# A fused attention and expert kernel: the transposed maxima of the scores go to the second score bank, one step sooner, and the expert masks ahead of the third maximum

## The reference

```
q = LN(x);  k = v = ctx;  rope(q), rope(k);  Q, K, V = 16 heads of 8
x = x + tanh(g_xattn) * (softmax(Q K^T / sqrt(8)) V Wo^T + bo)
z = LN(x);  xn = rmsnorm(z) * norm_scale;  s = xn Wr^T           # 8 experts
ids = top2(s);  c = softmax(s)[ids]
y = sum over ids of c * (up_val(xn) * silu(up_gate(xn))) Wdown^T   # hidden 352
x = x + tanh(g_ffn) * (y + z)
```

## Time and profile before

| | |
|---|---|
| median of 3 runs | 489.53 us |
| the profiled execution's own time | 488.46 us |
| its span (first to last instruction) | 486.7 us |
| granted TensorE clock, mean | 0.907 |
| TensorE busy | 395.8 us (81%) |
| VectorE busy | 300.7 us (62%) |
| ScalarE busy | 259.8 us (53%) |
| GpSimd busy | 249.0 us (51%) |

### The profile page before, as it was taken

The page is one execution under the profiler, slowest core; times in us unless marked ns, Lnnn a source line. Parts: engine busy times, 40 slices in busy tenths (PEclk is TensorE's granted clock), DMA queues, the critical chain, the costliest instruction groups (busy, mean ns, idle before and its releaser), DMA issues.

```text
span 486.7 us, 13346 instructions
## 1 busy us (share of the span) xinstructions
PE 395.8 (81%) x3788; PEld 269.2 (55%) x3789; DVE 300.7 (62%) x1112; ACT 259.8 (53%) x578; POOL 249.0 (51%) x205
## 2 busy tenths in 40 slices
PE   7578788888979788897987313999999999999960
PEld 3234445464655546455644202777777778777750
DVE  6377678788877887877773430555555555555440
ACT  3232658687676777785757301555455555545520
POOL 4464204136544565635344562456675665667574
PEclk9867899989899998998979555999999999999996
DMA  6331514037377703314011122334353443444230
GB/s 182 105 89 41 143 35 126 22 111 195 87 203 222 185 25 99 92 57 144 26 42 58 55 82 61 65 50 61 52 60 47 57 55 50 55 53 60 21 27 4
DMA packets 57413, 38.99 MB, mean 80 GB/s; under 512 B 8820, under 2 KB 55031, under 8 KB 57367
## 3 DMA queue, kind: packets, MB, share of 16 engines
q1 hardware_dynamic: 42614, 28.24, 22.0%
q0 software_dynamic: 12736, 8.64, 12.8%
q10 hardware_dynamic: 2016, 1.52, 1.2%
HBM read 14.29 MB, written 11.75 MB: 54 GB/s over the span
## 4 chain that ended last, share of the span: by engine, by line
PE 50%; DVE 16%; issue 10%; DMA 9%; ACT 4%; SPq 4%; POOL 3%; POOLq 2%; ACTq 1%; another core or an unknown queue 1%; DVEq 0%
DMA out<-ys,yi 7%; PE bank L1373 6%; PE bank L1351 6%; PE bank L1353 6%; DVE nmx L769 4%; PE bank L1176 4%; PE bank L1363 3%; SPq L237 3%; PE bank L1163 3%; PE bank L1097 2%; PE bank L1193 2%; PE bank L1150 2%; PE bank L1209 2%; ACT pt L542 2%; PE bank L1205 2%
## 5 line engine op out<-in xcount | busy, mean ns | idle before, releaser
L481 POOL DMA_INDIRECT out<-ys,yi x72 | 112.3, 1559 | 74.5 <-issue 37.1
L401 POOL DMA_INDIRECT slots_dram<-xr,slu x64 | 63.8, 997 | 69.3 <-ACT pt L542 47.5
L769 DVE TENSOR_REDUCE nmx<-bank 128x4 f32<-128x512 f32 x128 | 85.7, 676 | 11.9 <-PE bank L1150 11.5
L542 ACT ACTIVATE pt<-bank 128x512 f32<-128x512 f32 x128 | 72.9, 595 | 17.3 <-PE bank L1163 16.5
L1056 DVE TENSOR_TENSOR hh<-sg,bank 128x352 f32<-128x352 f32 x72 | 37.5, 521 | 54.3 <-PE bank L1353 39.3
L1373 PEld LDWEIGHTS bank<-wf_sb,hT 128*128 128x128 f32 (+1 forms) x432 | 56.7, 190 | 23.7 <-issue 19.8
L1373 PE MATMUL bank<-wf_sb,hT 128*128 (+1 forms) x432 | 61.0, 277 | 4.0 <-DVE hT L1066 4.0
L688 ACT ACTIVATE ys<-bank,yc 128x128 f32<-128x128 f32 x72 | 26.4, 367 | 63.7 <-PE bank L1373 33.4
L1351 PE MATMUL bank<-wf_sb,xT 128*128 x144 | 56.0, 471 | 0.0
L1176 PE MATMUL bank<-pt,v 128*9 128x128 f32 x1024 | 50.8, 282 | 6.1 <-ACT pt L542 5.3
L1353 PE MATMUL bank<-wf_sb,xT 128*128 x144 | 55.0, 464 | 0.0
(11 more groups left out here) (163 smaller groups left out, 708.2 us busy)
## 6 DMA issues: line engine op xcount, KB each, us to landing
qs<-parts SPq DMA_DIRECT2D x48, 128.0 KB
ks<-parts SPq DMA_DIRECT2D x42, 128.0 KB
xs<-slots_dram SPq DMA_DIRECT2D x72, 66.0 KB
wf_sb<-in_wup SPq DMA_DIRECT2D x8, 352.0 KB
x_sb<-in_x SPq DMA_DIRECT2D x8, 256.0 KB, 3.3
ctx_sb<-in_ctx_in SPq DMA_DIRECT2D x8, 256.0 KB
out<-x_sb SPq DMA_DIRECT2D x8, 256.0 KB
out<-ys,yi POOLq DMA_INDIRECT x72
```

What stands on the lines that cost most here:

```text
L401: nc.gpsimd.indirect_dma_start(out=slots_dram, out_offset=bass.IndirectOffsetOnAxis(ap=slu[:, c % 2, k, kk:kk + 1], axis=0), in_=xr[:, c % ...
L481: nc.gpsimd.indirect_dma_start(out=out.rearrange("b s d -> (b s) d"), out_offset=bass.IndirectOffsetOnAxis(ap=yi[:, r:r + 1], axis=0), in_ ...
L542: nc.scalar.activation(pt[:, 4 * g:4 * g + 4, :], STB[g % 2][:, :].rearrange("p (h s) -> p h s", h=4), ACT.Exp, scale=SCORE_SCALE).then_in ...
L769: nc.vector.tensor_reduce(nmx[:, b % 2, at:at + 4], SB[g % 2][:, :].rearrange("p (h s) -> p h s", h=4), AX.X, ALU.max, negate=True).then_i ...
```

## The change

The transposed maxima get another place, rows 0 to 15 and columns 0 to 127 of SB[1]. TensorE transposes the maxima of b + 2 at the end of step b, after the last weighted values and ahead of `project_out(b - 1)`, instead of those of b + 1 behind the scores near the step's start. VectorE makes the two copies right behind maximum 3 of the same batch. New waits follow: group 1 of the scores waits for the copies of the batch before (`d_mT`), and `transpose_attended` waits for `add_attention` of the batch before; the old waits of `transpose_maximum` on `add_attention` and of `transpose_attended` on `d_mT` go. SP issues the maxima of b + 2 at the end of its step. Ahead of the loop the maxima of batch 1 are transposed, copied and sent too.

On VectorE `choose_masks` and `choose_sum` (u = 0) move ahead of `maximum(b + 2, 2)`; `take_positions` and `take_scores` move ahead of `add_attention`, and `widen` (u = 3) behind it; the two copies stand ahead of `rotate_q` (u = 1).

```diff
-        mT_ps = SMALL[0:NH, 256:384]
+        mT_ps = SB[1][0:NH, 0:S]
...
 (SP)        maxima(0)
             sp.wait_ge(zeroed, 6)
+            maxima(1)
...
-                if real(b + 1):
-                    maxima(b + 1)
                 if u == 0 and there(c + 1):
                     stack_q_low(c + 1)
                     stack_k_high(c + 1)
                     stack_k_low(c + 1)
                 if 8 <= b < 8 + E:
                     ffn_weights(b - 8)
+                if real(b + 2):
+                    maxima(b + 2)
...
 (VectorE)   for g in range(4):
                 maximum(1, g)
+            maximum_high(1)
+            maximum_low(1)
...
                 if real(b + 2):
                     maximum(b + 2, 0)
-                if real(b + 1):
-                    maximum_high(b + 1)
-                    maximum_low(b + 1)
...
+                if u == 0 and there(c - 2):
+                    choose_masks(c - 2)
+                    choose_sum(c - 2)
                 if real(b + 2):
                     maximum(b + 2, 2)
-                if u == 0 and there(c - 2):
-                    choose_masks(c - 2)
+                if real(b + 2):
+                    maximum(b + 2, 3)
...
-                if u == 0 and there(c - 2):
-                    choose_sum(c - 2)
                 if real(b + 2):
-                    maximum(b + 2, 3)
+                    maximum_high(b + 2)
+                    maximum_low(b + 2)
                 if u == 1 and there(c + 2):
                     rotate_q(c + 2)
-                if u == 3 and there(c + 3):
-                    widen(c + 3)
-                if real(b - 1):
-                    add_attention(b - 1)
                 if u == 0 and there(c - 2):
                     take_positions(c - 2)
                 if u == 3 and there(c - 1):
                     take_scores(c - 1)
+                if real(b - 1):
+                    add_attention(b - 1)
+                if u == 3 and there(c + 3):
+                    widen(c + 3)
...
 (TensorE)       if 4 * b + g > 1:
                     pe.wait_ge(d_max, 4 * b + g - 1)
+                if g == 1 and b:
+                    pe.wait_ge(d_mT, b)
...
             def transpose_maximum(b):
                 pe.wait_ge(d_max, 4 * b + 4)
-                if b >= 3:
-                    pe.wait_ge(d_x1, b - 2)
...
             def transpose_attended(b):
                 pe.wait_ge(d_on, b + 1)
-                pe.wait_ge(d_mT, min(b + 3, B))
+                if b:
+                    pe.wait_ge(d_x1, b)
...
-            pe.wait_ge(d_bo, 8)
             transpose_maximum(0)
             for g in range(4):
                 scores(1, g)
+            transpose_maximum(1)
+            pe.wait_ge(d_bo, 8)
...
-                if real(b + 1):
-                    transpose_maximum(b + 1)
...
                     weighted_values(b, 3)
+                if real(b + 2):
+                    transpose_maximum(b + 2)
                 if real(b - 1):
                     project_out(b - 1)
```

## The result

The changed kernel took 503.37 us (median of 4 runs, 496.38 to 506.81); the kernel before took 489.61 us beside it. The ratio is 1.0226, with a 95% interval of 1.0159 to 1.0293: slower by some 2%, where I forecast 1.3% faster. The ratio rests on the faster runs (496.38 and 500.91); the profiled execution is a slower one, 506.81 us with a span of 505.0, so I use its trace for places and waits and not for the size of the loss.

A forecast was written before the change was run, and what follows sets the result against it. The prediction took the loop as bound by turns by TensorE and VectorE, ScalarE close behind, with about 20 us of movable TensorE waits. Its terms summed to -6.6 us off a median of 489.53: 482.9 us, range 478.5 to 490.5.

The forecast's parts named there:

- rotate_q: +1.6: VectorE, u = 1: `rotate_q` behind the copies sometimes meets GpSimd's `rotate_k`; a quarter of 6 x 1.1 us, +1.6 us.
- Rival B: GpSimd takes the gain back: `rotate_q` meets `rotate_k` in four rounds (4.4 us), no clock gain; 487.6 us, chance 0.18.
- Rival C: Each step's end: VectorE idles while TensorE transposes, 8.3 us in place of 2.8; slower, 493.9 us, chance 0.12.
- my sign of C: What would show Rival C: VectorE idle before the copies by over 8 us in total.
- The transposition (-3.8): TensorE's transposition of the maxima no longer waits for `add_attention`; half of 7.6 us comes back, -3.8 us.
- copies (-1.7): VectorE's two copies leave the step's head; half the 3.4 us scores wait for maxima comes back, -1.7 us.
- masks (-2.4): Masks ahead of the third maximum at u = 0 come sooner: 0.4 us for six rounds, -2.4 us.
- rival D: ScalarE is next: oT is ready no sooner and holds all 7.6 us and the clock; 487.8 us, chance 0.14.
- New waits (+2.8): Each step's output product queues behind maximum 3, at u = 2 behind the statistics, +2.8 us; scores 1's wait costed at nothing.
- SP's queue (-0.8): DMA issue in the loop: maxima of u = 2 leave before store and loads, so the second DMA wait goes, -0.8 us.
- Start (-1.2): Ahead of step 2: maxima of batch 2 land sooner, warming starts 0.95 us later; net -1.2 us.
- Clock (-1.1): Low-clock u = 0 steps of rounds 3 and 5: one of the two regains full clock, -1.1 us.

The follow-up runs named there:

- e4: The kernel before with only `rotate_q` moved behind `add_attention` in step u = 1: 504.10 us, ratio 1.0350.
- e1: The changed kernel with GpSimd's `rotate_k(n)` waiting until `rotate_q(n)` is done (n >= 2): 487.09 us, ratio 0.9956 to the kernel before.
- e10: e4 with GpSimd's `rotate_k` waiting for `rotate_q` as in e1: 490.34 us, ratio 1.0025 to the kernel before.
- e5: e1 with the expert weights issued in steps u = 2 and 3 of rounds 2 to 5, not steps 8 to 15: 483.23 us, ratio 0.9878.
- e2: The changed kernel with `rotate_q` put ahead of the two copies in step u = 1: 486.45 us, ratio 0.9998 to the kernel before.
- e9: The kernel before with both side edits of e5 (`rotate_k` waiting, weights moved) and nothing of the change: 487.44 us, ratio 0.9967.
- e8: e5 with `choose_masks` and `choose_sum` back behind maximum 2: 485.53 us, ratio 0.9955 to the kernel before.

## Why the prediction was wrong

**rotate_q: +1.6, the step that failed.** It failed in the start, in the price and in the reader. I wrote that `rotate_q` "starts up to 0.5 us later relative to the step". Against the output product it started 1.0 to 1.3 us later in rounds 2 to 5 (0.09 us behind it before, 1.39 in round 2 after). I priced a meeting with `rotate_k` at 1.1 us for one half, from the single meeting of before. In rounds 2 to 5 GpSimd ran both of its halves at once, and VectorE's half outlasted them: up to 3.58 us, 2.9 more than its 0.67. And I named no reader of it, though `project_q` waits for `rotate_q` directly (`d_q`) and stands in the very next step; TensorE's 12.1 us of waiting and the lower clock behind it were in no term. All six steps met, not a quarter. `rotate_q` came later by the wait for the transposition and two copies, and GpSimd's `rotate_k` 0.3 to 0.5 us sooner against the product in rounds 2 to 4 (2.0 in round 5). I took GpSimd's distance of "about a microsecond" for a property of GpSimd's; it hung on `rotate_q` being ahead of the second scatter (e4). e1, e4 and e10 show this step alone: moved without the change it costs 3.5%, and one wait on GpSimd takes the loss away from either kernel. Step 10 alone is no clean measure of it: in e1 it still takes 3.0 us more than before, behind the DMA of the maxima. Steps 14, 18 and 22 are: 12.27, 11.73 and 11.49 us in the changed kernel, 8.67, 7.43 and 8.44 in e1.

Rival B had the mechanism and too small a price (4.4 us, its ceiling 6.6), for the same reason. Rival C had the sign by the wrong mechanism. VectorE did stand idle in front of the copies (16.9 us, my sign of C was 8), but it had stood idle there for the output product before, and e5 has 14.5 us of it and is faster; the sign was a bad one.

**Who gives way.** The Trainium skill, SBUF — State Buffer, section "Who interferes with whom", was the warning, and its first half holds: two tensor inputs on VectorE against a GpSimd instruction that reads. That the one issued first keeps its way for a whole instruction (from which, too, it does not follow that `shift` would always lose, as I wrote) does not fit the starts in these rows: VectorE began 0.20 us (e4) and 0.53 us (after) before GpSimd and still finished behind two of GpSimd's instructions. The measurement decides. Other rows do fit: in round 1 of e2 the second half of `rotate_q` kept its 0.69 us and GpSimd's first took 2.01 instead of 1.27. Where VectorE lost although it began first, GpSimd's half came straight behind a scatter; in e2 GpSimd had been waiting for ScalarE. What decides is open.

**The transposition (-3.8), copies (-1.7), masks (-2.4).** Together -7.9 forecast. The waits for `add_attention` fell to zero and the wait for oT grew by only 2.0 us (2.4 to 4.4, over 40 to 290), so rival D does not hold. Those for the masks fell by more than half in the changed kernel, and in e5 by a third (8.5 to 5.7, over 40 to 290). With both losses out, the change is worth 4.3 us (e5 against e9), about two thirds of my whole sum of 6.6. The mechanism fits; the sizes of the three terms were not separated.

**New waits (+2.8): wrong place, near in size by luck.** I had maximum 3 behind the statistics at u = 2. The diff puts maximum 3 right behind maximum 2, so the transposition almost never waited for it (0.8 us, once, ahead of the loop). What stands behind the statistics are the copies, and scores 1 wait for them: 3.6 us in nine steps, where I had costed "nothing".

**SP's queue (-0.8): wrong sign.** The wait for the maxima grew where TensorE came sooner: 2.46 us in step 10 of e1. I looked at what is issued in front of the maxima, not at what must land before them.

**Start (-1.2): nearly nothing.** From the first scores to the scores by key of step 2 it took 57.93 - 34.80 = 23.1 us before, and 58.61 - 35.72 = 22.9 after. The DMA wait of 2.30 us went, but the twelve warming matmuls took 5.33 us instead of 3.97, behind two idle stretches of TensorE for maxima. (Before, the maxima of batch 2 were issued behind nine stack DMAs of their step, not eleven.)

**Clock (-1.1).** The u = 0 step of round 5 lost its low clock (6.63 us, before 8.80), that of round 3 kept it (8.16 us at 0.79), as "one of the two" had it; but it came back at u = 2, behind the longer waits (0.74 in step 10), and in round 5 already at u = 1: that step ran at 0.62 and took 9.00 us, before 6.51 at 1.00.

## What to carry to other kernels

Before an operation with two SBUF inputs is moved on VectorE, list GpSimd's tensor operations of the same stretch with their distance, and move both in thought: here one came 1.0 to 1.3 us later and the other 0.3 to 0.5 sooner. Ask too what makes the distance; it may hang on the very order that is about to change, as it did here on the scatter. Follow each moved result to every reader by its semaphore, the next step's too. And where a stage gets faster, look for what was hidden only because the consumer came late (here a DMA behind 352 KB of weights): it can take the gain back until it is moved as well.

## What was not expected of the hardware

A VectorE multiplication of 128x512 f32 that takes 0.67 us alone took 3.25 and 3.58 us beside two GpSimd multiplications of 1.27 us each, though it had begun first; GpSimd's took no longer than alone in these rounds (in rounds 0 and 1 its second half took 1.72). GpSimd's indirect DMAs did VectorE no harm: in e1 this half took 0.67 us (from 110.14) with a scatter running from 109.67 to 110.67. The harm went the other way: a scatter that began beside `rotate_q` took up to 2.16 us instead of 1.0 (e8; in e1 2.15 us from 170.48, `rotate_q` from 170.51 to 171.78). The kernel before differed by 1.8% between chips (481.0 to 489.6 us).
